# Attention in a fused transformer block: value products moved behind the scores, output projection moved ahead of the third transposes

## What is computed

```
ln = _ln(_layernorm(x))                       # 2048 tokens x 256
q, k, v   = fp8 projections of ln             # 16 query heads, 8 key/value groups, 128 wide
qx        = fp8 projection of ln              # 16 heads
kx, vx    = split(ctx @ w_kv_x)
q, k, qx, kx = _ln per head
core = softmax(q k^T / sqrt(128)) v           # within a sequence of 64 tokens
xout = softmax(qx kx^T / sqrt(128)) vx
cat  = fp8 quantise(concat(core, xout) / smooth)
x = x + (cat @ wproj) * scale
x = x + moe_ffn(_layernorm(x))
```

## Time and profile before

| | |
|---|---|
| time, median of 3 runs | 925.39 us (925.27 to 927.94) |
| the profiled execution, its own time | 924.58 us |
| its span, first to last instruction | 922.5 us |
| mean granted TensorE clock over the span | 0.995 |
| TensorE busy | 885.3 us, 96% |
| VectorE busy | 740.6 us, 80% |
| ScalarE busy | 673.7 us, 73% |
| GpSimd busy | 497.8 us, 54% |

### The profile page before, as it was taken

One profiled execution on the slowest core, in us unless ns is written; L12 is line 12 of the kernel. 1 busy time (PEld: TensorE's weight loads), 2 busy tenths in 40 slices (PEclk: granted clock), 3 DMA queues, 4 the chain that ended last, 5 costly groups with the idle time before them and its releaser, 6 DMA issues.

```text
span 922.5 us, 22025 instructions
## 1 busy us (share of the span) xinstructions
PE 885.3 (96%) x7812; PEld 594.9 (64%) x7812; DVE 740.6 (80%) x1498; ACT 673.7 (73%) x1182; POOL 497.8 (54%) x509
## 2 busy tenths in 40 slices
PE   5689999999999999999999999999999999999996
PEld 2365667777777777777776776666665565665554
DVE  6789999899999999999999999988699864333332
ACT  6998888888888888888888888885455654444443
POOL 5336766575666775765756666640107632343444
PEclk9989999999999999999999999999999999999999
DMA  9943301001000100110010001031536776888865
GB/s 204 336 120 70 70 25 53 30 31 47 30 30 25 53 30 24 33 45 31 30 47 30 30 25 53 25 121 52 178 121 211 239 196 126 126 139 131 141 103 63
DMA packets 96104, 80.07 MB, mean 87 GB/s; under 512 B 67968, under 2 KB 84096, under 8 KB 95872
## 3 DMA queue, kind: packets, MB, share of 16 engines
q1 hardware_dynamic: 86544, 64.09, 26.0%
q0 software_dynamic: 9456, 14.59, 8.9%
HBM read 50.41 MB, written 18.68 MB: 75 GB/s over the span
## 4 chain that ended last, share of the span: by engine, by line
PE 81%; DVE 11%; ACT 4%; issue 2%; POOL 1%; DMA 0%; POOLq 0%; DVEq 0%; ACTq 0%
PE b_pj L354 25%; PE b_tr L373 9%; PE b_o L414 7%; PE b_sc L385 7%; PE b_acc L457 5%; PE b_pj L1393 5%; PE b_o L1430 5%; PE b_o L1517 3%; PE b_pt L404 3%; PE b_sc L1393 3%; PE b_tr L1393 3%; PE b_pj L1470 2%; PE b_sc L1470 1%; PE b_tr L1470 1%; DVE a L1805 1%
## 5 line engine op out<-in xcount | busy, mean ns | idle before, releaser
L731 POOL TENSOR_TENSOR rstd<-vareps,neghalf 128x4 f32<-128x4 f32 (+1 forms) x128 | 176.2, 1377 | 10.7
L724 POOL TENSOR_SCALAR vareps<-ssq,unit 128x4 f32<-128x4 f32 (+1 forms) x128 | 71.5, 558 | 199.4 <-DVE ssq L543 199.2
L354 PE MATMUL b_pj<-w_hi,xq 128*128 128x512 f16 x384 | 147.7, 385 | 1.1 <-DVE xq L713 0.9
L354 PE MATMUL b_pj<-w_lo,xq 128*128 128x512 f16 x384 | 147.3, 384 | 0.0
L469 ACT ACTIVATE sq<-b_pj 128x512 f32<-128x512 f32 x192 | 115.8, 603 | 40.7 <-PE b_pj L354 39.3
L543 DVE TENSOR_REDUCE ssq<-sq 128x4 f32<-128x512 f32 x192 | 130.5, 680 | 14.1 <-ACT sq L469 12.6
L373 PE MATMUL b_tr<-ident,nrm 128*128 128x128 f32 x768 | 119.6, 278 | 7.5 <-DVE nrm L554 3.2
L1376 POOL DMA_INDIRECT out<-xn x39 | 61.1, 1566 | 109.6 <-ACT xn L1588 46.4
L482 ACT ACTIVATE raw<-b_pj 128x512 f32<-128x512 f32 x192 | 117.5, 612 | 0.0
L373 PEld LDWEIGHTS b_tr<-ident,nrm 128*128 128x128 f32 x768 | 90.1, 141 | 38.4 <-issue 6.7
L502 ACT ACTIVATE qT<-b_tr,col,hw 128x512 f32<-128x512 f32 x128 | 100.8, 787 | 1.5 <-PE b_tr L373 1.5
(11 more groups left out here) (329 smaller groups left out, 2028.5 us busy)
## 6 DMA issues: line engine op xcount, KB each, us to landing
nst<-in_ffw SPq DMA_DIRECT2D x40, 512.0 KB, 3.3
wload<-in_ffw SPq DMA_DIRECT2D x20, 512.0 KB
xbuf<-zero SPq DMA_DIRECT2D x13, 387.0 KB, 9.6
x_sb<-in_x SPq DMA_DIRECT2D x4, 512.0 KB, 14.1
wproj<-in_ctxT SPq DMA_DIRECT2D x1, 2048.0 KB, 10.8
xhl<-in_w_all SPq DMA_DIRECT2D x4, 512.0 KB, 18.8
wproj<-in_wprojT POOLq DMA_DIRECT2D x4, 512.0 KB, 5.3
rowbuf<-xr SPq DMA_DIRECT2D x16, 128.0 KB, 1.8
```

What stands on the lines that cost most here:

```text
L354: last = pe.matmul(o, x, w[kind][:, k, at:at + BANK], start=(k == 0 and n_ == 0), stop=(k == KT - 1 and n_ == len(terms) - 1))
L731: pool.tensor_tensor(rstd[:, r % 2, c, :], vareps[:, r % 2, c, :], neghalf[:, 0:1].unsqueeze(2).to_broadcast(shape), ALU.pow)\
```

## The change

Two entries of TensorE's list move. The value products of slot N-1 now come directly behind the scores of slot N+1 (before, between the second transposes and project 2), and the output projection of slot N-2 comes between project 2 and the third transposes (before, behind the third transposes). The value products of slot 0 get one wait more, for the end of the weight preparation, whose last matmuls use the same banks. Nothing is added to or taken from the computation, and the other engines' lists stay as they are.

```diff
             def pe_values(pe, N):
                 r = SLOTS[N][1]
+                if N == 0:
+                    pe.wait_ge(s["wlo_done"], len(UNITS))
                 pe.wait_ge(s["ptev_done"], N + 1)
...
                 run_slots(pe, [
                     (1, pe_scores, "scores"),
+                    (-1, pe_values, "values"),
                     (2, pe_transpose(0), "first transposes"),
...
                     (2, pe_transpose(1), "second transposes"),
-                    (-1, pe_values, "values"),
                     (3, pe_project(2), "project 2"),
+                    (-2, pe_out, "out"),
                     (2, pe_transpose(2), "third transposes"),
-                    (-2, pe_out, "out"),
                     (3, pe_project(3), "project 3"),
```

## The result

The changed kernel takes 933.56 us (median of 5 runs, 933.25 to 934.5), the kernel before 925.27 in the same comparison. The ratio is 1.0087, 95% interval 1.0068 to 1.0105: 8.3 us slower, where 919.0 and a gain was forecast; it lies above the range of 912.5 to 924.8. The profiled execution has a span of 931.4 us, 8.9 more than before.

A forecast was written before the change was run, and what follows sets the result against it. TensorE's own instructions were taken as the bound, without gaps in steady state. 924.58 - 5.6 (division) - 2.0 (covered waits) + 1.2 (scores' wait) = 918.2 us profiled, 919.0 as median; range 912.5 to 924.8.

The forecast's parts named there:

- Saving by fewer changes of division: TensorE, iterations 1 to 62: three changes of array division instead of four, 0.09 us saved each, 5.6 us in all.
- no emptying between scores and values: Rival, chance 0.14: going from scores to values empties nothing on TensorE, so another 5.6 us is gained: 913.4 us.
- two prices in one: Rival, chance 0.14: scores to values costs what two changes did, or a hidden weight load shows: 924.6 us.
- Output projection ahead of the third transposes: TensorE, same undivided steps in another order: costed at nothing, bounds 0 to 2 us.
- Why out was moved with the values: Otherwise third transposes come 0.44 + 0.87 us after the second, whose eviction starts 0.70 behind them and lasts 0.77.
- The scores' wait for the third eviction: Scores in 15 short iterations without token transposes: 1.48 us needed, 1.40 filled, 0.08 lost each, 1.2 us in all.
- Other waits of the moved steps: Values find the probabilities' eviction ready some 0.5 us early; slot 0's added wait costs nothing; VectorE's loop keeps some 0.7.
- Waits outside the steady state: TensorE waits at the start, 592.50 and 627.88, partly covered by the moved values: 0 to 3.5 us gained, 2.0 taken.
- The slower rival: Chance 0.10: ScalarE reaches the third eviction late, delaying scores in 31 short iterations; 0.4 us late gives 930.2 us.
- The signs that the prediction named: For being wrong: scores below 1.0 or 1.17 and more; TensorE waiting on ScalarE in all iterations, or for VectorE's `nrm`.

The follow-up runs named there:

- e5: Kernel of e1 with the value products ahead of the scores instead of behind them: 918.44 us, ratio to the kernel before 0.9924.
- e4: Kernel before with only the output projection moved ahead of the third transposes, values left in their old place: 941.33 us, ratio 1.0177.
- e3: Changed kernel with the output projection put back behind the third transposes, so only the values are moved: 949.1 us, ratio 1.0255.
- e1: Changed kernel with the eviction of the transposed probabilities ahead of the third eviction in ScalarE's list: 922.71 us, ratio to the kernel before 0.9981.
- e7: Changed kernel with the values ahead of the scores, the probabilities' eviction left behind the third eviction: 945.17 us, ratio 1.0214.
- e6: Kernel of e1 with the values moved from behind the scores to behind project 0: 928.47 us, ratio to the kernel before 1.0042.

## Why the prediction was wrong, point by point

*Saving by fewer changes of division: right.* 0.09 in each of 62 iterations was forecast. The second transposes went from 0.53 to 0.44. In e5, whose steady state has one wait, of 0.3 us, four iterations are 0.42 shorter than before, 0.105 each, a little more than forecast; the changed kernel is as much shorter than e4. Neither "no emptying between scores and values" nor "two prices in one" happened: the scores kept 1.08 up to the values. The Trainium skill, page "TensorEngine Tiling (Array Packing)", section "Key Properties", says that a change of tiling mode drains TensorE. The traces agree as far as a price can show it: three changes cost 0.105 an iteration less than four, and one between scores and values costs about as much as any other. That it is a drain no run shows.

*Output projection ahead of the third transposes, "I cost it at nothing": wrong, and this is the step that failed.* The steps themselves cost the same in either order. What the prediction listed as waiting for the third transposes' eviction was the scores (0.08, 15 times). It left out what stands behind that eviction in ScalarE's list and who else waits for that: the eviction of the probabilities, and behind it the token and row transposes, which write its bank. It worked that eviction's time out, 0.66 + 0.60 later, but only for the values. Of the iteration with token transposes it said that the scores' wait "is covered" there; it took the token transposes as work that covers, and did not read what they themselves wait for (`ptev_done`, in `pe_token_T` and `pe_rows`). It could have been had from rows of the kernel before: third transposes to the eviction's start 0.70, then 0.66 to the next, 0.60 for it: 1.96, against 0.44 and 0.87 of work in front, so 0.65 lost once in four iterations. In the wide one 0.44 and 1.30 stand in front, so 0.2. Each grows by the 0.14 that passed between the eviction's end and the transposes' start. Measured against before, the two iterations are 0.67 and 0.21 longer; with the 0.09 saved taken in, that is 0.76 and 0.30 of waiting. Per four iterations that is 1.06, and over 13 such about 14 us. It is e4 that shows it alone, with 0.77 and 0.31, and 15.9 us above before. The 8.3 us measured are this loss less what moving the values gave back.

*Why out was moved with the values: right in place, too small in size.* The prediction wrote that without it the third transposes would come only 1.31 behind the second, against 0.70 and 0.77 for the eviction, which makes 0.16. e3 shows that wait, at 0.50 an iteration: the 0.70 was read at the third eviction, while the second starts 0.87 behind its transposes, and 0.15 more passes behind its end.

*The scores' wait for the third eviction: right in place and size.* 0.08 in short iterations without token transposes was forecast; 1.46 instead of 1.40 was measured, 0.06. In e1, where ScalarE does 0.48 of work more in front of it, it is 1.57.

*Other waits of the moved steps: right.* The values waited nowhere in the steady state; VectorE's loop did not become the bound.

*Waits outside the steady state, 2.0 taken: about 1.3.* The wait at 592.50 was covered: from scores to scores that iteration took 9.44 (587.97 to 597.41), and takes 8.57 now (597.70 to 606.27). The wait at 627.88 is gone too: from the last scores to the end of the span are 296.9 us, where it was 298.3. At the start the waits moved on, as a part was expected to. The last two scores got new ones, 0.33 and 0.87, and at 597.41 two small matmuls into `b_pt` waited 0.58 as the token transposes do; in front of the last scores the output projection alone had stood between them and the third transposes, and now nothing does. Timeline of TensorE in the changed kernel:

```profile
96.41 1.15 PE L385 MATMUL b_sc<-kT,qT 128*64 128x64 f32 x32 [0.55 <-ACT qT L504]
...
102.49 0.66 PE L373 MATMUL b_tr<-ident,nrm 128*128 128x128 f32 x4 [0.66 <-DVE nrm L556]
...
634.48 1.15 PE L385 MATMUL b_sc<-kT,qT 128*64 128x64 f32 x32 [0.87 <-ACT qT L504]
```

The scores that began at 107.80 begin at 106.85, and some 0.4 of that is the saving of the iterations before. Without that saving, and from start to start, 0.6 was covered at the start, 0.8 at 592.50 and 1.3 behind the last scores; 1.4 came back in the two iterations up to the last scores.

*The slower rival, with its 930.2 the nearest to the 933.56 measured, named the right engine and the wrong mechanism; that it comes near is luck.* It let ScalarE come late to the third eviction and priced the scores' wait. ScalarE wasn't late: it had 0.17 us idle in front of that eviction. The work it does behind it was late, because it stood behind it. The signs that the prediction named don't describe this: the scores' waits stayed below 0.1, and the waits on ScalarE's evictions came in two iterations of four, not in all.

## What to carry to other kernels

Where a step is moved ahead of another on one engine, follow the result of the one that now comes later through the list of the engine that takes it over: everything behind that eviction is delayed as well, and each reader and each next writer of its buffers, the rare steps that were counted as cover among them, is a wait to be checked. When a reordering on one engine loses a little, look for the matching move on the other engine before giving it up: one entry of ScalarE's list turned 933.6 into 922.7 us, and with values ahead of scores into 918.4.

## What the runs showed of the hardware

A step of transposes that had waited for a ScalarE eviction started 0.14 to 0.15 us behind its end (412.17 to 412.31 in the changed kernel, 418.30 to 418.45 in e3), whereas scores and values started 0.05 behind the one they had waited for (scores: 420.39 and 0.78 give 421.17, to 421.22 in the changed kernel, and 633.65 and 0.78 give 634.43, to 634.48; values: 427.68 and 0.59 give 428.27, to 428.32 in e7). The timeline of weight loads in the changed kernel shows a load of the transposes at 412.28, 0.03 ahead of the matmuls, and the scores' at 421.22, with them. So the time between load and matmul is at most 0.03 of the difference; what makes the rest is open. Changing the array's division cost 0.09 at the entry from an undivided step, whether the new one divides rows (0.31 instead of 0.22 ahead of the values in e6) or columns (project 3 in 0.96 instead of 0.87 ahead of the scores in the kernel before), and four transposes that follow a divided step directly took 0.49 instead of 0.44. One change less in an iteration gave 0.105.
